# A short memset after each gather on GpSimd, and one weight load moved behind ten ring releases

## The reference

```python
msg = edge_val[:, None] * feat_in[edge_col]
aggr = jax.ops.segment_sum(msg, edge_row, num_segments=feat_in.shape[0])
aggr = aggr + (1.0 + eps) * feat_in
h = jnp.maximum(aggr @ W1 + b1, 0.0) @ W2 + b2
h = jnp.maximum(h, 0.0)
...
```

## Time and profile before

| what | value |
|---|---|
| runs shown | 1272.94, 1275.2, 1278.61 us; median 1275.2 us |
| profiled execution | 1274.54 us, span 1272.8 us |
| mean granted TensorE clock | 0.829 |
| busy: PE, weight loads, DVE | 893.7, 613.4, 735.5 us |
| busy: ACT, GpSimd | 679.8, 661.5 us |
| edge stage, first gather to GpSimd's first add L741 | 104.02 to 763.37 us |

### The profile page before, as it was taken

The page is one execution under the profiler, slowest core; times in us unless marked ns, Lnnn a source line. Parts: engine busy times, 40 slices in busy tenths (PEclk is TensorE's granted clock), DMA queues, the critical chain, the costliest instruction groups (busy, mean ns, idle before and its releaser), DMA issues.

```text
span 1272.8 us, 26947 instructions
## 1 busy us (share of the span) xinstructions
PE 893.7 (70%) x6929; PEld 613.4 (48%) x6930; DVE 735.5 (58%) x1653; ACT 679.8 (53%) x2186; POOL 661.5 (52%) x673
## 2 busy tenths in 40 slices
PE   2383288566666465654777765884369999999995
PEld 1131143234333232332566544774357787777883
DVE  4674178565866455564555565896835555555553
ACT  7884199327685267852333412663335555555552
POOL 3835666464665666656666419120525454454442
PEclk9995599767897678887656778895589999999998
DMA  4114222234222332323444312363012322322322
GB/s 123 62 48 135 87 82 78 61 92 100 85 87 75 92 87 84 90 77 91 134 145 151 111 54 93 102 190 111 1 59 42 49 44 47 49 43 48 50 42 25
DMA packets 59620, 102.56 MB, mean 81 GB/s; under 512 B 10298, under 2 KB 43048, under 8 KB 59400
## 3 DMA queue, kind: packets, MB, share of 16 engines
q0 software_dynamic: 29520, 65.96, 21.1%
q1 hardware_dynamic: 30008, 35.55, 8.7%
HBM read 84.27 MB, written 17.20 MB: 80 GB/s over the span
## 4 chain that ended last, share of the span: by engine, by line
PE 45%; DVE 17%; ACT 10%; issue 8%; another core or an unknown queue 8%; DVEq 2%; DMA 1%; POOL 0%; POOLq 0%; ACTq 0%
PE bank L1055 7%; ACT Wall L1141 6%; PE bank L1041 4%; PE bank L1043 4%; PE bank L1042 4%; PE bank L896 4%; PE bank L894 3%; PE bank L1057 3%; ACT RB L1149 3%; DVE RA L1633 3%; PE bank L907 3%; PE bank L895 3%; PE bank L858 2%; DVE Wall L1633 2%
## 5 line engine op out<-in xcount | busy, mean ns | idle before, releaser
L726 POOL DMA_INDIRECT Wall<-xl_d,gbuf x391 | 388.5, 994 | 272.1 <-SPq L595 147.2
L1149 ACT ACTIVATE RB<-RB,gbuf 128x128 f16<-128x128 f16 x488 | 178.8, 424 | 283.9 <-DVE RB L1620 259.6
L894 PE MATMUL bank<-Wall,RB 128*128 x488 | 165.7, 339 | 139.9 <-DVE Wall L1633 54.1
L1141 ACT ACTIVATE Wall<-Wall 128x128 f32<-128x128 f16 (+1 forms) x782 | 247.1, 383 | 26.7 <-DVE Wall L1548 25.2
L1633 DVE TENSOR_TENSOR RA<-RA,bank 128x256 f32 x244 | 101.8, 417 | 253.0 <-remote 127.8
L1271 ACT ACTIVATE RA<-bank,b1T 128x128 f32<-128x128 f32 x448 | 127.7, 368 | 121.1 <-PE bank L1043 119.6
L786 POOL DMA_INDIRECT out_dram<-RA,slot_tok x56 | 99.7, 1780 | 162.3 <-ACT RA L1277 138.0
L858 PE MATMUL bank<-Wall 128*128 128x512 f16 (+1 forms) x391 | 153.7, 440 | 39.1 <-ACT Wall L1141 26.0
L1041 PE MATMUL bank<-RA,Wall 128*128 128x128 f16 x896 | 175.4, 221 | 0.4 <-issue 0.2
L1043 PE MATMUL bank<-RA,Wall 128*128 128x128 f16 x896 | 175.3, 221 | 0.0
L1042 PE MATMUL bank<-RA,Wall 128*128 128x128 f16 x896 | 175.2, 221 | 0.0
(11 more groups left out here) (319 smaller groups left out, 1585.2 us busy)
## 6 DMA issues: line engine op xcount, KB each, us to landing
stage<-in_L_ffn_W SPq DMA_DIRECT2D x10, 1024.0 KB
Wall<-xl_d,gbuf POOLq DMA_INDIRECT x391
Wall<-in_L_ffn_W SPq DMA_DIRECT2D x6, 1024.0 KB, 6.5
Wall<-in_x SPq DMA_DIRECT2D x4, 640.0 KB, 7.4
xl_d<-Wall SPq DMA_DIRECT2D x4, 640.0 KB
out_dram<-RB SPq DMA_DIRECT2D x4, 640.0 KB
xn_d<-RA SPq DMA_DIRECT2D x4, 640.0 KB
RB<-in_x SPq DMA_DIRECT2D x1, 1792.0 KB
```

Of the source, the lines that this page charges most:

```text
L726: pool.indirect_dma_start(out=ring[:, t % RING * 2 * D:(t % RING + 1) * 2 * D], out_offset=None, in_=xl_d, in_offset=bass.IndirectOffsetOn ...
L894: mm(o, high, ring[:, bass.ds(at, D)], start=True, stop=False)
L1141: last = act.activation(hi_word[:, n % SR, k * S:(k + 1) * S], hi_hot[:, n // HB % 2, n % HB // 2, 0:S, n % 2], ACT.Copy, scale=pay[k][:, ...
L1149: act.activation(low, high, ACT.Copy, scale=rec_r[:, n:n + 1]).then_inc(sw_built, 1)
```

## The change

Two edits.

After every gather, GpSimd runs a memset over `pause`, columns 442 to 511 of the scratch tile `small` (128 partitions x 70 columns of fp32), which nothing reads. It goes through `link`, a helper that the kernel has already: the instruction raises `pool_step` and the engine waits for that step before it goes on.

`w1_tile`, the tile ahead of whose release the load of W1 stands on SP, becomes `EC` = 391 for the last expert. No release has that number, so the load comes out of the loop behind all of them.

```diff
+        pause = small[:, at + P:]
+        assert at + P < 4 * P
...
         def w1_tile(e):
 
-            return (T0[1] + 12, T0[-1] - 8)[e] if e < 2 else T0[-1] + 10 * e - 9
+            return (T0[1] + 12, T0[-1] - 8)[e] if e < 2 else T0[-1] + 10 * e - 9 if e < NE - 1 else EC
...
                     ).then_inc(gathered[t % RING], 16)
+                    link(pool.memset(pause, 0.0))
```

## The result

The change made the kernel slower by about half a per cent: 1281.11 us (median of 15 runs, 1276.0 to 1285.74) against 1273.97 before (15 runs), ratio 1.0056 with a 95% interval of 1.0043 to 1.0069. The forecast was 1230 us, 3.5% faster, with 1198 to 1320 as its range. The time lies inside the range; the direction was wrong.

A forecast was written before the change was run, and what follows sets the result against it. Close gathers on GpSimd were taken to stall PE, DVE and SP. With a 1.56 us period L741 would come 45 us earlier: 1274.5 - 45 = 1229.5, plus 0.7 to the median, 1230 us; range 1198 to 1320.

The forecast's parts named there:

- the relief: Edge stage: with gathers spaced out the stalls go, DVE's remote waits falling from 127.8 us to under 40.
- the tail: From the last gather's end to GpSimd's add L741: 4 us, where 26.8 us stood before.
- What bounds the kernel: Edge stage, 104 to 764 us: gathers following each other at 1.25 us make PE's progress reach DVE and SP late.
- The period with the pause: GpSimd, from gather to gather: 0.994 + 0.30 + 0.155 + 0.06 + 0.05, so 1.56 us where back to back it was 1.25.
- the hand-over: GpSimd, from the gather to the added memset: another 0.05 us in the period.
- The lower end of 1.51: GpSimd's period without the hand-over; gathers would end at 694 and L741 start at 698, 65 us less.
- The contrast: Stretch 318 to 367 us: 33 gathers, one per 1.48 us, and no add of DVE waits longer than 1.8 us.
- The other work of a chunk: Chunks 1, 2 and 3 less remote waits: 139, 132 and 159 us, under GpSimd's 162, 162 and 161.
- The moved load: Expert 7's load on SP, behind the last release: alone 4 us saved, no term of its own in the sum.
- The signs: Changed profile if right: gathers 0.95 to 1.0 us, remote waits under 40, slot waits under 50, L741 at about 718.
- rival 1: No relief: the pause doesn't end the stalls and memsets only cost, 1327 us, 1379 with nothing hidden; chance 0.22.
- rival 2: Partial relief or a dearer pause: period 1.65 to 1.75, or a third of stalls stay; 1257 to 1287 us; chance 0.20.

The follow-up runs named there:

- wide memsets: Changed kernel with its pause memset as 140 fp16 or 175, 200, 225 or 280 one-byte elements: ratios 0.9937, 0.9821, 0.9826, 0.9911, 1.0020 to the kernel before.
- 280-byte kernel: Changed kernel, load moved, its memset as 280 one-byte elements instead of 70 fp32: ratio 1.0020 to the kernel before.
- 175- to 225-byte kernels: Changed kernel, load moved, its memset as 175, 200 or 225 one-byte elements: ratios 0.9821, 0.9826 and 0.9911 to the kernel before.
- 200-byte kernel: Changed kernel, load moved, its memset as 200 one-byte elements instead of 70 fp32: 1252.9 us, ratio 0.9826 to the kernel before.
- half_row: Kernel before, each gather fetching 128 rows of 512 B instead of 1 KB: 1269.4 us against 1264.15 before.

## Why the prediction was wrong, point by point

The 45 us of gain failed at three steps: the new period, 1.397 us instead of 1.56; the relief, which was read from a stretch that doesn't show it and isn't there at 1.40; and the end of the gathers with the tail behind them, which come 48 us later than said even in a kernel with the forecast's period and without its stalls.

**What bounds the kernel: right.** Gathers that follow each other closely hold PE, DVE and SP up. Taking them out took 164 us off and every remote wait; spacing them by 1.5 us took the remote waits from 127.8 to 10.8. By what way gathers do it, no run shows.

**The period with the pause: wrong, and so this kernel kept its stalls.** The step was the sum 0.994 + 0.30 + 0.155 + 0.06 + 0.05 = 1.56. Of its terms, the memset is 0.171 instead of 0.155. The wait on its own step (0.06) and the hand-over (0.05) were added to the gather's 0.30, but all three are one stretch of 0.27. And 0.994 is the mean of a gather, with the stretched ones in it, while the median is 0.954. So 0.954 + 0.171 + 0.27 = 1.395, and the median spacing measured is 1.397. The lower end of 1.51 was 0.11 too high as well, because it too used the mean and kept the 0.30 and the 0.06 apart. The four idle operations don't add to the spacing either. A shorter pause than forecast was bad news here, since the spacing was its effect. But this isn't the whole miss: at the forecast's own period the gain isn't there either, as the pace and the tail below show.

**The contrast: misread.** The stretch of 318 to 367 us was taken as gathers 1.48 us apart without a stall, and so as the sign that 1.56 is safe. 1.48 is a mean. The gathers there stand in runs of 3 to 8, most of them 1.25 us apart, with idle stretches of 0.8 to 1.6 us between the runs; the median spacing is 1.25, as in the stalls. The timeline of GpSimd before:

```profile
327.95 0.95 POOL L726 DMA_INDIRECT Wall<-xl_d,gbuf  x1 [0.30 <-SPq L595]
329.20 0.95 POOL L726 DMA_INDIRECT Wall<-xl_d,gbuf  x1 [0.30 <-issue]
330.45 0.95 POOL L726 DMA_INDIRECT Wall<-xl_d,gbuf  x1 [0.30 <-issue]
332.76 1.38 POOL L726 DMA_INDIRECT Wall<-xl_d,gbuf  x1 [1.36 <-SPq L595]
```

So the trace didn't say which even spacing is enough, or that spacing alone decides. The wide memsets say it afterwards: 1.40 isn't enough, and at 1.50 the remote waits are all but gone.

**The pace and the tail: two terms too small.** The 280-byte kernel runs at the forecast's own spacing, 1.568, with its stalls gone (remote 11.0 of 127.8). It is the forecast's world, and its ratio is 1.0020 instead of 0.965. Two terms of the sum are to blame. First, 391 gathers don't go at their shortest spacing: the mean spacing is 1.641, and of the 0.073 above 1.568 gathers stretched beyond their median of 0.951 make (1.012 - 0.951) x 391 = 24 us. The sum had the stretching in it, as 0.994, but counted the wait and the hand-over besides the 0.30; that the sum agrees with this kernel's median spacing is luck, for its memset is 0.345 and not 0.155. The last gather ends at 745.5, where 714 was said. Second, the tail: 4 us were taken, 20.2 were measured, and about 20 in the 175- to 225-byte kernels. Together the two make 48 us, against a forecast gain of 45.

```profile
744.59 0.95 POOL L728 DMA_INDIRECT Wall<-xl_d,gbuf  x1 [0.27 <-POOL small L732]
745.55 0.34 POOL L732 MEMSET small<- 128x280 uint8 x1
765.77 1.40 POOL L744 TENSOR_TENSOR RA<-RA,Wall 128x256 f32<-128x256 f32 x2 [19.88 <-DVE Wall L1636]
```

The reason stands in the code, and could have been read there. Step i of a chunk waits for tile i, a chunk has 103 tiles but 128 steps, so 25 steps always follow the last gather. In the 200-byte kernel the last gather ends at 729.37. PE, idle on a gather's data for 4.33 us, takes up the last tile but one at 732.90 and the last at 733.81. The 25 steps behind it, at about 0.52 us of DVE for each add (13 us) and with DVE's other work between, end at 749.4. The timeline of PE there:

```profile
732.90 0.39 PE L897 MATMUL bank<-Wall,RB 128*128 x1 [4.33 <-DMA Wall<-xl_d,gbuf]
```

The 26.8 us of tail in the earlier trace rows were read as backlog of the stall. That some 20 of them are these steps' own is inferred from the kernels without a stall.

**The other work of a chunk as 139, 132 and 159 us: near.** With chunk 0's 101 (205 - 104) these make 531 us. Without gathers GpSimd's first add starts at 600.88, 497 us after 104, so taking off the remote waits alone left 34 us too much. The order of the two was right: GpSimd's pace is late once the stalls are gone, as PE's 91.1 us of waits for gathers at 200 bytes show.

```profile
600.88 6.88 POOL L739 TENSOR_TENSOR RA<-RA,Wall 128x256 f32<-128x256 f32 x10 [27.07 <-DVE Wall L1631]
```

**The moved load: right in size and place.** 4 us were taken, 4.1 measured alone. Also right: the load isn't held up by its new place, since w_done 14 releases it in either; the product that needs it waited 8.39 us (under 9 was said), and no idle time of GpSimd in chunk 3 is over 5 us. Beside the pause it was no term of its own, and it gave nothing, but the reason that was given, that GpSimd's pace sets the end, wasn't so in this kernel.

**The signs.** Of those named, gathers of 1.032 us on the mean (0.95 to 1.0 was said), remote waits of 101.9 us (under 40 was said), slot waits of 72.8 (under 50), the first gather of chunk 1 at 241.5 (229) and L741 at 776.19 (718) all say that the forecast failed.

**The rivals.** By its picture the result is nearest to rival 1, no relief: the stalls stand and the memsets only cost. But it put 52 us on the clock and 7 came, since GpSimd's instructions between two gathers added 0.15 us, not 0.265 (57 us in all, with 74 us of slot waits to take it), and gave its mark as remote waits over 110 us, while 101.9 were measured. By its number the result is in rival 2's 1257 to 1287, but by neither of its ways: the period was not 1.65 to 1.75, and four fifths of the remote waits stayed, not a third. The rule of the Trainium skill that was weighed (page "SBUF — State Buffer", section "Who interferes with whom") says that only the shared port pair makes engines contend; read as the prediction did, it means that a pause on GpSimd can free nothing. The wider pauses don't bear that out: 0.28 us of memset took the remote waits from 127.8 to 10.8 us, and PE did 139 matmuls in the stretch where it had done 30. Whether ports have a part in the stalls, no run tells. Nor is the price one of bytes, by half_row. The sign came out as rival 1's, but not for its reason, that spacing doesn't matter.

## What to carry to other kernels

When one engine's instructions hold the others up by following each other too closely, a pause can have a narrow optimum, as here: too small it costs and gives nothing, too large it is the pace. Size it by sweeping it, in steps of a few hundredths of a microsecond, before judging the idea; a single point says little either way. Look at each spacing in a stretch that is taken as the good example, not at their mean. And work out the pace and the tail that remain when the stall is gone, from the code's own dependences, before booking the stall as gain.

## What the runs showed of the hardware

- Indirect gathers on GpSimd that follow each other at 1.25 us added 164 us to this kernel, 0.42 us each, and gathers of half the bytes or half the rows ran no faster (1269.4 and 1277.1 us against 1264.15). Two memsets in place of each added 11.6 us (1120.0 against 1108.4). By which way gathers do it is open.
- From 1.40 to 1.50 us of spacing the stalls go away. PE's granted clock in 130 to 155 us is 0.50 (1.2 GHz) up to 1.40, with 30 to 51 matmuls done, 0.83 and 0.80 at 1.45 and 1.49, and 1.00 (2.4 GHz) at 1.50, with 139.
- Four idle linked operations behind a gather don't add to the spacing: it is 1.255 us with them and 1.251 without (the kernel's time did rise, to 1283.5 us). With two or four linked memsets behind each gather, the next one starts 0.28 us later where it also has a wait on `tile_free` ahead of it; with one memset it doesn't.
- A memset on GpSimd goes by its elements, not its bytes: 70 fp32 took 0.171 us, 140 fp16 0.228, 280 one-byte 0.345, these three over the same 280 bytes per partition.
